# Rotated queries by head, u on column halves, and full-precision scores of two heads on row halves

## The reference, cut to what matters

```python
q_hk = (hidden_q @ Wq.T).reshape(Bv, Sv, H, K)
q_big = jnp.einsum('bshk,hkq->bshq', q_hk, w_kc_q)      # 192 per head
q_big = _apply_rope(q_big, sin_q, cos_q)                # x*cos + rotate_half(x)*sin, halves of 96
kv_r = _apply_rope(kv_c, sin_k, cos_k)
q_r = jnp.einsum('bshq,hqr->bhsr', q_big, W_qr)
k_r = jnp.einsum('bld,hdr->bhlr', kv_r, W_kr)
scores = jnp.einsum('bhsr,bhlr->bhsl', q_r, k_r)
attn = jax.nn.softmax(scores, axis=-1)
ctx_c = jnp.einsum('bhsl,bld->bhsd', attn, kv_r)
```

## Time and profile before

| | |
|---|---|
| runs | 469.98, 470.81, 470.88 us (median 470.81) |
| profiled execution | 468.11 us, span of the core 466.3 us |
| busy in the span | PE 88%, DVE 67%, ACT 46%, POOL 39% |
| mean granted clock of TensorE | 0.978 of full |
| loop of groups | about 33 to 285 us of the span |

### The profile page before, as it was taken

One profiled execution on the slowest core, in us unless ns is written; L12 is line 12 of the kernel. 1 busy time (PEld: TensorE's weight loads), 2 busy tenths in 40 slices (PEclk: granted clock), 3 DMA queues, 4 the chain that ended last, 5 costly groups with the idle time before them and its releaser, 6 DMA issues.

```text
span 466.3 us, 5952 instructions
## 1 busy us (share of the span) xinstructions
PE 408.9 (88%) x1991; PEld 262.6 (56%) x1997; DVE 310.8 (67%) x681; ACT 214.5 (46%) x562; POOL 184.0 (39%) x149
## 2 busy tenths in 40 slices
PE   1989999999999999999899998287772987999997
PEld 1766666676666766666567784133341453533475
DVE  4898768665776566767787656188799856574322
ACT  1336646665566646654578533058850124321100
POOL 1496554555445655545452349670001200040000
PEclk9999999999999999999999999699898899999999
DMA  8752020200201100003000051000000000000011
GB/s 317 263 188 84 1 91 1 77 17 0 91 0 37 55 1 1 1 5 121 1 0 2 1 114 47 0 0 1 1 1 0 0 1 1 0 1 0 1 45 45
DMA packets 8941, 18.82 MB, mean 40 GB/s; under 512 B 2128, under 2 KB 6672, under 8 KB 7760
## 3 DMA queue, kind: packets, MB, share of 16 engines
q1 hardware_dynamic: 8912, 18.46, 11.5%
HBM read 17.40 MB, written 1.05 MB: 40 GB/s over the span
## 4 chain that ended last, share of the span: by engine, by line
PE 56%; DVE 27%; issue 5%; POOL 5%; ACT 4%; DMA 3%; SPq 1%; DVEq 0%; ACTq 0%
PE bank L1146 6%; PE bank L1395 5%; PE bank L1413 5%; PE bank L1159 5%; PE bank L1085 4%; PE bank L1183 4%; PE bank L1189 4%; PE bank L1171 4%; PE bank L1087 3%; PE bank L1086 3%; DVE rot_z L752 3%; PE bank L1279 3%; DVE uT L777 2%; DVE tail_all L1006 2%; PE bank L1106 2%
## 5 line engine op out<-in xcount | busy, mean ns | idle before, releaser
L418 POOL TENSOR_TENSOR prob<-prob,rinv 128x512 f32<-128x512 f32 x64 | 67.7, 1057 | 103.2 <-DVE rinv L818 101.1
L562 ACT ACTIVATE prob<-bank,negmax 128x256 f32<-128x256 f32 x128 | 59.5, 471 | 51.5 <-DVE negmax L813 51.4
L813 DVE TENSOR_REDUCE negmax<-bank 128x2 f32<-128x512 f32 x64 | 44.0, 688 | 29.8 <-PE bank L1159 29.4
L392 POOL TENSOR_TENSOR c_y<-c_ve,minus_half 128x4 f32<-128x4 f32 (+1 forms) x10 | 12.4, 1243 | 97.3 <-DVE c_ve L699 69.9
L1159 PE MATMUL bank<-kvT,uT 128*128 128x256 f32 x256 | 46.4, 303 | 0.4 <-issue 0.4
L413 POOL TENSOR_TENSOR rot_low<-rot_low,rot_up 128x1024 f32<-128x1024 f32 x16 | 38.7, 2419 | 16.4 <-DVE rot_up L746 16.2
L1395 PE MATMUL bank<-tailT,blobs 128*128 128x512 f32 (+1 forms) x96 | 42.7, 597 | 1.8 <-ACT tailT L505 0.8
L1279 PE MATMUL bank<-wfc,ident 128*128 128x512 bf16 x139 | 36.5, 411 | 7.3 <-DVE xs L921 6.7
L1085 PE MATMUL bank<-xnT,w 128*128 128x512 f32 x96 | 40.2, 419 | 2.8 <-DVE rot_z L752 2.4
L553 ACT COPY probT<-bank 128x512 f32<-128x512 f32 x64 | 37.4, 585 | 9.3 <-PE bank L1171 8.6
L1159 PEld LDWEIGHTS bank<-kvT,uT 128*128 128x128 f32 x256 | 34.5, 189 | 12.5 <-issue 12.3
(11 more groups left out here) (188 smaller groups left out, 757.1 us busy)
## 6 DMA issues: line engine op xcount, KB each, us to landing
blobs<-in_blob SPq DMA_DIRECT2D x8, 1024.0 KB, 6.1
xs<-in_x SPq DMA_DIRECT2D x2, 512.0 KB, 4.1
ctxT<-in_ctx_t SPq DMA_DIRECT2D x1, 1024.0 KB, 13.2
xn<-in_w_fc_t SPq DMA_DIRECT2D x1, 1024.0 KB, 5.1
ctxT<-in_w_proj_t SPq DMA_DIRECT2D x1, 1024.0 KB, 5.6
out<-qk SPq DMA_DIRECT2D x8, 128.0 KB, 1.7
cb<-in_const_b SPq DMA_DIRECT2D x1, 768.0 KB, 9.0
blobs<-in_w_gate SPq DMA_DIRECT2D x1, 704.0 KB, 4.3
```

Source lines behind the costliest of these rows:

```text
L418: pool.tensor_tensor(p[:], p[:], rinv[:, n % PROBS, :].unsqueeze(2).to_broadcast([P, 2, S]), ALU.mult).then_inc(normed, 1)
L562: ins = act.activation(prob[n % PROBS][:, st, :], pS[n % 2][:, st * S:(st + 1) * S], ACT.Exp, bias=negmax[:, n % 2, st:st + 1], accum_out= ...
```

## The change

1. The query rows are sorted by head: r=0 and r=1 each hold 64 rows of the first half and 64 of the second half of one head, r=2 the leftovers of both heads. Every rope is now one operation of 128 rows and two of 64 rows that cross partitions; every join is 512 columns; constants and weights are permuted to fit.
2. The u of head h from its own rows is one matmul of 128 x 64 on column half h (two instructions, the halves side by side), and only the shared rows r=2 need a full one.
3. u is copied by ACT in one operation of 128 x 512 and not split; `u_low`, the key split and their waits go. Scores of two heads are made together in slots k=0 and k=3, in full precision, head h from rows 64h to 64h+63 of u and keys, into `pS[h]`. They wait for the exponentials of both units before.

```diff
-                if z:
+                if r == 2:
                     pool.tensor_tensor(rz[:, 0, :], rz[:, 0, :], rz[:, 1, :], ALU.add).then_inc(joined, 1)
                 else:
-                    pool.tensor_tensor(low, low, up, ALU.add).then_inc(joined, 1)
+                    pool.tensor_tensor(low[:, r, :], low[:, r, :], up[:, r, :], ALU.add).then_inc(joined, 1)
...
-                for h in range(2):
-                    lo, hi = h * DC, (h + 1) * DC
-                    ins = act.copy(uT[n % 2][lo:hi, h, :], pu[lo:hi, :])
-                ins.then_inc(u_high, 1)
+                act.copy(uT[n % 2][:], pu[:]).then_inc(u_copied, 1)
...
-                    dve.tensor_tensor(tokens(low[:, 0, :]), tokens(src[:]), angles(cosq, 0), ALU.mult)
-                    ins = dve.tensor_tensor(tokens(low[:, 1, :]), tokens(src[:]), angles(sinq, 0), ALU.mult)
...
+                straight, crossed = (low[:, r, :], up[:, r, :]) if r < 2 else (rz[:, 0, :], rz[:, 1, :])
+                dve.tensor_tensor(tokens(straight), tokens(src[:]), angles(cosq, r), ALU.mult)
+                for lo, to in ((0, DC), (DC, 0)):
+                    ins = dve.tensor_tensor(tokens(crossed[to:to + DC, :]), tokens(src[lo:lo + DC, :]),
+                                            angles(sinq, r, lo, lo + DC), ALU.mult)
...
-                if s % 2 == 0 and m % RT == 2 and m // RT - 1 < GROUPS:
-                    u_low(m // RT - 1)
...
-                pe.matmul(pu[:], wqk[f % 2][:, r * P:(r + 1) * P], rz[:, 0, :] if r == 2 else low[:, r, :],
-                          start=(r == 0), stop=(r == RT - 1)).then_inc(u_ready, 1)
+                if shared:
+                    pe.matmul(pu[:], wqk[f % 2][:, P:2 * P], rz[:, 0, :], start=False, stop=True).then_inc(u_ready, 1)
+                    return
...
+                for h in range(2):
+                    ins = pe.matmul(pu[h * DC:(h + 1) * DC, :], wqk[f % 2][:, h * DC:(h + 1) * DC], low[:, h, :],
+                                    start=True, stop=False)
...
-                if n >= 2:
-                    pe.wait_ge(probs_ready, n - 1)
+                if n:
+                    pe.wait_ge(probs_ready, n)
...
-                    for i in range(2):
-                        ins = pe.matmul(pS[n % 2][:, st * S:(st + 1) * S], uT[b // 2][:, h, at:at + P],
-                                        kvT[i][:, b * S:(b + 1) * S], start=(i == 0), stop=(i == 1))
-                ins.then_inc(scores_ready, 1)
+                    for h in range(2):
+                        lo, hi = h * DC, (h + 1) * DC
+                        ins = pe.matmul(pS[h][:, st * S:(st + 1) * S], uT[b // 2][lo:hi, at:at + P],
+                                        ktmp[lo:hi, b * S:(b + 1) * S], start=True, stop=True)
+                        if st == 1:
+                            ins.then_inc(scores_ready, 1)
```

More of the change, by code:

```diff
@@ L175, in build @@
             w1 = [[part(f"w1_{j}_{i}", [P, DK, 2 * DCQ]) for i in range(2)] for j in range(2)]
-            wqk = [part(f"wqk_{j}", [P, RT * P], F32) for j in range(2)]
-            uT = [part(f"uT_{j}", [P, 2, CH]) for j in range(2)]
-            kvT = [part(f"kvT{i}", [P, TOK]) for i in range(2)]
+            wqk = [part(f"wqk_{j}", [P, 2 * P], F32) for j in range(2)]
+            uT = [part(f"uT_{j}", [P, CH], F32) for j in range(2)]
             rot_low = [part(f"rot_low{j}", [P, 2, CH], F32) for j in range(2)]
@@ L285, in w1_parts_of @@
         def w1_parts_of(w, i, folded):
-            quarters = folded[:, 0:2 * DCQ].rearrange("p (u n) -> p u n", u=2)
-            return ((w[:, i, 0:2 * P].rearrange("p (u n) -> p u n", u=2), quarters[:, :, 0:P]),
-                    (w[:, i, 2 * P:3 * P].rearrange("p (u n) -> p u n", u=2), quarters[:, :, P:DCQ]))
+            heads = folded[:, 0:2 * DCQ].rearrange("p (h u n) -> p h u n", h=2, u=2)
+            shared = w[:, i, 2 * P:3 * P].rearrange("p (u h n) -> p h u n", u=2, h=2)
+            return ((w[:, i, 0:2 * P].rearrange("p (h u n) -> p h u n", h=2, u=2), heads[:, :, :, 0:DC]),
+                    (shared, heads[:, :, :, DC:HALF]))
         def w8_piece(j):
@@ L443, in _ @@
             pool.memset(pad, 0.0).then_inc(kva_ready, 1)
-            join(1, 1)
+            join(1, 2)
             for s in range(SLOTS, LAST + 1):
@@ L449, in _ @@
                     norm_probs(unit_at(s - 1))
-                if s % 2 == 1 and m < ALLQ and m % RT:
-                    join(m // RT, m % RT - 1)
+                if s % 2 == 1 and m < ALLQ:
+                    join(m // RT, m % RT)
             pool.wait_ge(d_small, 16)
@@ L515, in fold_copy @@
                 elif i == 2:
-                    act.copy(wqk[f % 2][:], pW[:, 0:RT * P]).then_inc(wqk_ready, 1)
+                    act.copy(wqk[f % 2][:], pW[:, 0:2 * P]).then_inc(wqk_ready, 1)
                 else:
@@ L736, in rope @@
                 src = q_bank(m)
-                if r == 0:
-                    if n >= 2:
-                        dve.wait_ge(u_ready, RT * (n - 2) + 2)
-                    dve.tensor_tensor(tokens(low[:, 0, :]), tokens(src[:]), angles(cosq, 0), ALU.mult)
-                    ins = dve.tensor_tensor(tokens(low[:, 1, :]), tokens(src[:]), angles(sinq, 0), ALU.mult)
[L742 to L753, removed]
+                if r == 0 and n >= 2:
+                    dve.wait_ge(u_ready, 2 * (n - 2) + 1)
+                if r < 2 and n:
+                    dve.wait_ge(joined, RT * (n - 1) + r + 1)
+                if r == 2 and n >= 2:
+                    dve.wait_ge(u_ready, 2 * (n - 1))
+                straight, crossed = (low[:, r, :], up[:, r, :]) if r < 2 else (rz[:, 0, :], rz[:, 1, :])
[3 more added lines that the diff above has]
+                                            angles(sinq, r, lo, lo + DC), ALU.mult)
                 ins.then_inc(rot_ready, 1)
@@ L772, in _ @@
             dve.wait_ge(d_cb, 16)
[L773 to L779, removed]
             rope(0)
@@ L1110, in prep @@
                     blob_f = wb[f % NBLOB]
-                    for r in range(RT):
-                        ins = pe.matmul(pW[:, r * P:(r + 1) * P], blob_f[:, C_QR + r * P:C_QR + (r + 1) * P],
-                                        blob_f[:, C_KR:C_KR + P], start=True, stop=True)
+                    for r, (lo, hi) in enumerate(((0, DC), (DC, P), (0, P))):
+                        at = 0 if r < 2 else P
+                        ins = pe.matmul(pW[:, at + lo:at + hi], blob_f[:, C_QR + r * P:C_QR + (r + 1) * P],
+                                        blob_f[:, C_KR + lo:C_KR + hi], start=True, stop=True)
                 else:
@@ L1227, in _ @@
             prep(1, 1)
-            for r in range(RT):
-                latent_u(0, r)
+            latent_u(0, 0)
+            latent_u(0, 1)
             prep(1, 2)
@@ L1233, in _ @@
                 m, f, slot = s // 2, s // SLOTS, s % SLOTS
-                if unit_at(s) is not None:
+                if unit_at(s) is not None and unit_at(s) % 2 == 0:
                     if unit_at(s) == 0:
-                        pe.wait_ge(kv_parts, 1)
+                        pe.wait_ge(kv_ready, 1)
                     scores(unit_at(s))
@@ L1426, in tables @@
     sin_q, cos_q = sincos(DCQ)
-    low = np.concatenate([np.arange(HALF), np.arange(P - HALF)])
-    rest = np.arange(P - HALF, HALF)
+    own, rest = np.arange(DC), np.tile(np.arange(DC, HALF), 2)
     cos_t, sin_t = cos_q.T, sin_q.T
-    cos_rows = [cos_t[low], cos_t[low + HALF], np.concatenate([cos_t[rest], cos_t[rest + HALF]])]
-    sin_rows = [sin_t[low + HALF], -sin_t[low], np.concatenate([sin_t[rest + HALF], -sin_t[rest]])]
+    cos_rows = [np.concatenate([cos_t[i], cos_t[i + HALF]]) for i in (own, own, rest)]
+    sin_rows = [np.concatenate([sin_t[i + HALF], -sin_t[i]]) for i in (own, own, rest)]
     const_b = np.concatenate(cos_rows + sin_rows, axis=1)
```

52 lines of the change are left out of this document (21 added, 31 removed).

## The result

The changed kernel takes 477.13 us (median of 4 runs, 476.95 to 477.58) against 470.39 for the kernel before (4 runs, 468.94 to 470.88): ratio 1.0153, 95% interval 1.0134 to 1.0171. It is slower by about 7 us. The profiled execution of after took 477.12 us with a span of 475.3, that of before 468.11 and 466.3, so the two traces differ by 9.0 us.

The account below looks back on a forecast made before the run. PE was taken as the bound, busy 158.6 of 164.7 us. Start +2.4, odd groups +4.3, even +1.4, end -1.1 make +7.0 on the median 470.8: 477.8, less 1.0 for rounding: 476.8 us, range 472.5 to 482 (chance 0.55).

Parts of the forecast that it names:

- The mechanism it named: In odd groups, PE's prep 2 waits about 1.4 us for `w1_low`, behind DVE's rope of 2.13 instead of 1.21.
- Odd group to the scores of units 2 and 3: From an odd group's first q to these scores on PE: 8.21 us against 7.29 before, +0.92.
- From there to the next q: From the scores of units 2 and 3 to the next group's first q: 7.67 us against 7.87.
- the chain on ACT: Exponentials and copies between scores and context: context 5.58 us after the scores, where PE alone would be there at 5.2.
- The loop: The steady groups: six odd ones +4.3 us in all, five even ones +1.4.
- rounding: ACT durations and prep 2's wait were rounded up, by up to 0.2 us a group over eleven; 1.0 taken off.
- Start: Before the loop, longer DVE ropes delay the first q by 1.1 us; the first group takes 1.3 more; +2.4 together.
- End: SP's loads after the last scores start earlier, since these come a slot earlier with unit 2's: -1.1 us.
- Rival 1: Score row halves on PE run one after the other: 0.86 us more for each of 32 pairs, about 503; chance 0.12.
- Rival 2: Faster: crossing operations overlap the rope's first on DVE, rope 1.6 instead of 2.13 us, total 461; chance 0.17.
- Rival 3: Half the waits appear: prep 2's is absorbed at the context, shape switches cost half; 471 to 472 us, chance 0.16.
- The price of a changed shape: PE's cost of switching array shape: 0.16 us for a change to 64 columns, 0.21 for any other.

Follow-up runs that it names:

- experiment 1: The changed kernel with the one call `w1_low` moved ahead of the rope on DVE: 470.17 us.
- experiment 5: The changed kernel with the load of the third fold's weights issued first in SP's queue, ahead of the wait for the keys' sum: 476.95 us.
- Experiment 10: The changed kernel with DVE's two scans of feed-forward weights cut to 256 of 2048 columns (475.00 us) or, in a second kernel, moved two slots later (474.35 us).
- the same half of the change: Rows by head, three-operation ropes, u on column halves; with all moves in both kernels, 460.55 us without this half against 455.97 with it.
- 2: The first half alone (rows by head, three-operation ropes, u on column halves), split scores, `u_low` and key split kept as before: 481.82 us.
- 4: The changed kernel with `w1_low` and both negmax of a pair ahead of the rope, u's copy behind the probabilities' copy: 459.32 us, ratio 0.9767.
- 6: The changed kernel with `w1_low` and both negmax of a pair ahead of the rope, the copy of u left in place: 463.90 us.

## Why the prediction was right, and where its sum was off

The prediction was 476.8 us, slower. The mechanism it named is what runs: prep 2 was forecast to wait about 1.4 us for `w1_low` and waits 1.40; ropes last 2.13; PE's own work fell; ACT's chain took the place of the third rope's wait; and experiment 1 gives back the loss by moving what prep 2 waits for. The agreement of the total is closer than that of its terms.

- **Odd group to the scores of units 2 and 3**: forecast 8.21, measured 182.51 - 174.31 = 8.20.
- **From there to the next q**: forecast 7.67, measured 7.46 in odd groups and 7.41 in even ones. The failed step is the chain on ACT. I had added durations; the trace gives starts:

```profile
168.79 0.48 ACT L558 ACTIVATE prob<-bank,negmax 128x256 f32<-128x256 f32 x1 [1.40 <-DVE negmax L792]
...
169.71 0.58 ACT L530 COPY uT<-bank 128x512 f32<-128x512 f32 x1
170.17 0.60 ACT L549 COPY probT<-bank 128x512 f32<-128x512 f32 x1
170.65 0.50 ACT L558 ACTIVATE prob<-bank,negmax 128x256 f32<-128x256 f32 x1
...
171.58 0.59 ACT L549 COPY probT<-bank 128x512 f32<-128x512 f32 x1
```

  Two exponentials are 0.92 and 0.93 (I took 0.99), the copy of u 0.46 (0.59). With 1.89 to the first exponential, which was right, and 0.65 behind the copy, the context comes 5.33 after the scores, not 5.58. So an even group gained 0.07 where I had a loss of 0.27, and an odd one lost 0.50 instead of 0.72. The loop was summed to 4.3 + 1.4 = 5.7, less 1.0 for rounding; it is 6 x 0.50 - 5 x 0.07 = 2.7. Rounding was worth 3.0.
- **Start**: forecast +1.1 to the first q and +1.3 in the first group, measured +3.1 and +1.9. Of the 3.1, 0.9 lie ahead of the first rope and differ between executions. Two causes in the rest were not in the sum. Behind PE's idle time ahead of prep 2 came the lower clock, 1 us more for row scores at half speed. And the third fold's load is queued on SP behind the keys' sum, which the ropes delay; experiment 5 shows that only 0.6 us of the first group hung on it; the rest is DVE's.
- **A term that I missed**: the two scans. Before they cost 0.2 and 0.7 us (groups of 15.26 and 15.31 against 15.10 and 14.62), after 1.0 and 1.55; that is 1.7 us of the loss. Experiment 10 shows the 2.6 of after; the 0.9 of before is only read from the lengths of its groups.
- **End**: forecast -1.1, measured -1.3.
- **Sum**: between the traces I forecast 7.0 - 1.0 = 6.0 us, and 9.0 were measured: the start was under by 2.6 and the scans by 1.7, the loop over by 2.0, the end by 0.2, and 0.9 came in the two stretches of the feed-forward part, which the sum does not have. That the median came out within 0.4 us is part luck: the profiled execution of before (468.11) lies 2.3 below its median, that of after on it, so 9.0 between the traces are 6.7 between the medians, where I had carried the 6.0 over unchanged. The errors of the terms, which reach 2.6 us, cancelled.

Rival 1, row halves one after the other, is excluded: 1.07 us a pair and not 1.9. Rival 2, the faster one, held a true part: PE's own count is a gain, and it comes as soon as nothing waits. Its mechanism, overlapping crossed operations, did not occur (0.71 us from the rope's first operation to the crossed ones, 1.42 from there to what follows). Rival 3 fails at the wait of prep 2, which nothing absorbed. Its sum was wrong too: 8 x 0.1 is 0.8 us a group and not 0.4.

Of the rule that a weight load overlaps only where the row group differs (the Trainium skill, TensorE: Matmul & The Clock Gate, Part 3): taken alone, the runs speak against it here. The same part also lets a load into the array's background weight buffer go ahead; no run here tells whether that is what happens. Each row half's passes follow each other on the same row group, and the eight weight loads of one pair of scores, 0.19 us each, all start between 182.5 and 183.1, while its matmuls run. Four rounds take 1.07 us with the change of shape, the sum by hidden loads (0.11 + 0.86 + 0.10); with 0.11 more in each later round it would be 1.40.

## What to carry to other kernels

When a change makes one engine's operation longer and another engine's work shorter, look first at what stands behind the longer operation in that engine's own order: here one call moved ahead of a rope decided 7 us (3 of which it would have given the kernel before as well), and three moves turned +1.5% into -2.3% without touching a matmul. Make sums of a chain from starts and not from durations, and look for once-only work on it, since a chain that moves onto the path takes the cover of that work away. Judge a change of the arithmetic only after the order has been fitted to it: the same half of the change cost 2.6% alone in the old order and gained 1.0% in the new one.

## What I had not expected of the hardware

- Two idle stretches of PE, 1.62 and 0.46 us, were followed by 3 us at half the clock (granted 0.52 from 33 to 36 us), and eight passes took 2.0 instead of 1.07 us. With 0.37 and 0.46 us of idle time the clock stayed at 1.00. All eight traces with a wait of 1.6 us at this prep 2 show the lower clock behind it, for some 3 us in five of them and near 7 in three (after and experiments 1, 2, 4, 5, 6 and both of 10); the six without it, before among them with 1.10 and 0.35 us idle, show none. So a wait at such a place can cost more than its own length.
- Two full-precision matmuls of 64 rows, one on each row half, take together the time of one: eight passes of 256 columns in 1.07 us with the change of shape.
- The price of a changed shape was the same after row halves as after the column halves from which it was forecast: the first pass of a q starts the next one after 0.33 us (174.31 to 174.64) where 0.23 lie between two others, and two passes of the shared u take 0.97 us to the next start (167.96 to 168.93) instead of 0.85.
